# Row maxima handed over by halves of a head group, split on GpSimd, and a shorter lead of maximum units

## The reference

```
q = (x @ Wq.T).reshape(B, S, H, hd)      # B=4, S=1024, H=16, hd=8; k and v alike, q and k rotated
scores = jnp.einsum('bhqd,bhkd->bhqk', q, k) / math.sqrt(hd)
attn = jax.nn.softmax(scores, axis=-1)   # needs the maximum of each row of 1024 scores
ctx = jnp.einsum('bhqk,bhkd->bhqd', attn, v)
x = x + ga * (ctx @ Wo.T)
h = layernorm(x) * (1 + cb) + sb
_, idx = jax.lax.top_k(silu(h @ rw1 + rb1) @ rw2 + rb2, 2)     # routing to two of 8 experts
x = x + gb * (h + sum over the two experts of weight * (silu(h @ we1 + be1) @ we2 + be2))
```

## Time and profile before

| | us |
|---|---|
| median of 3 runs | 1115.19 |
| lowest and highest run | 1113.39, 1119.62 |
| span of the profiled execution | 1115.6 |
| busy: TensorE, VectorE, ScalarE, GpSimd | 905.9, 817.5, 726.9, 346.0 |
| first maximum unit on VectorE | 113.38 |
| first score matmul of the steps | 163.62 |
| first tile of the experts | 899.30 |

### The profile page before, as it was taken

How to read it: one execution, slowest core, us unless ns; L and a number is a source line. 1 busy time by engine, 2 the same in 40 slices (tenths; PEclk the granted TensorE clock), 3 DMA queues, 4 the chain that set the end, 5 groups by cost and what they waited for, 6 DMA issues and landing times. The chain is left out here.

```text
span 1115.6 us, 17986 instructions
## 1 busy us (share of the span) xinstructions
PE 905.9 (81%) x5934; PEld 362.1 (32%) x5934; DVE 817.5 (73%) x1141; ACT 726.9 (65%) x1580; POOL 346.0 (31%) x598
## 2 busy tenths in 40 slices
PE   2354459999999989898988988898898769869982
PEld 1222012222222222221212221222222168859972
DVE  3886988999999988877998798789871025613366
ACT  0043018888888878777887877788788646526651
POOL 1333000000000262043035205223323327666883
PEclk9667559999999989988998998899999779968997
DMA  4054430404402000071000000100000012112353
GB/s 123 0 196 179 162 129 1 149 16 152 158 25 105 30 2 29 23 198 49 1 30 6 25 30 25 44 1 30 1 1 13 27 44 61 54 60 68 102 146 111
DMA packets 57049, 72.69 MB, mean 65 GB/s; under 512 B 9504, under 2 KB 37664, under 8 KB 56960
## 3 DMA queue, kind: packets, MB, share of 16 engines
q1 hardware_dynamic: 52416, 62.21, 17.3%
q0 software_dynamic: 4544, 9.35, 2.4%
HBM read 30.08 MB, written 41.06 MB: 64 GB/s over the span
## 5 line engine op out<-in xcount | busy, mean ns | idle before, releaser
L860 DVE TENSOR_REDUCE half_max<-ps_max 128x2 f32<-128x1024 f32 x512 | 601.7, 1219 | 90.7 <-PE ps_max L676 71.6
L791 ACT ACTIVATE probs<-ps_scores 128x512 f32<-128x512 f32 x1024 | 540.1, 603 | 112.2 <-PE ps_scores L697 99.0
L710 PE MATMUL ps_ctx<-probs,v_grp 128*32 128x512 f32 x2048 | 286.5, 633 | 0.7 <-ACT probs L791 0.7
L697 PE MATMUL ps_scores<-q_set,k_set 51*128 51x512 bf16 x1024 | 261.2, 398 | 27.1 <-ACT probs L791 16.0
L676 PE MATMUL ps_max<-k_set,q_set 48*128 48x512 bf16 x1024 | 195.9, 409 | 70.4 <-DVE half_max L860 57.2
L697 PEld LDWEIGHTS ps_scores<-q_set,k_set 51*128 51x128 bf16 x1024 | 68.6, 94 | 347.9 <-ACT probs L791 304.1
L613 POOL TENSOR_TENSOR ctx<-turned,inv_sum 128x128 f32<-128x128 f32 x32 | 13.1, 410 | 375.7 <-DVE inv_sum L887 375.2
L1527 ACT ACTIVATE hid<-ps_up,w_tile 128x128 f32<-128x128 f32 x312 | 89.3, 370 | 58.5 <-PE ps_up L1693 53.3
L676 PEld LDWEIGHTS ps_max<-k_set,q_set 48*128 48x128 bf16 x1024 | 51.0, 96 | 177.8 <-DVE half_max L860 156.5
L1492 POOL DMA_INDIRECT y_rows<-y,y_to x78 | 91.6, 1174 | 48.9 <-DVE y L1564 32.9
L1564 DVE TENSOR_TENSOR y<-ps_down,w_tile 128x128 f32<-128x128 f32 x78 | 22.8, 292 | 104.0 <-PE ps_down L1703 58.9
(11 more groups left out here) (197 smaller groups left out, 658.0 us busy)
## 6 DMA issues: line engine op xcount, KB each, us to landing
slots<-zero_rows SPq DMA_DIRECT2D x43, 387.0 KB, 6.0
q_terms<-parts SPq DMA_DIRECT2D x24, 256.0 KB, 2.5
k_terms<-parts SPq DMA_DIRECT2D x24, 256.0 KB, 3.2
q_set<-q_terms SPq DMA_DIRECT2D x32, 192.0 KB
k_set<-k_terms SPq DMA_DIRECT2D x32, 192.0 KB
slots_in<-slots SPq DMA_DIRECT2D x78, 64.5 KB
rows<-y_rows SPq DMA_DIRECT2D x16, 256.0 KB
w_all<-in_we SPq DMA_DIRECT2D x1, 2048.0 KB
```

Source lines behind the costliest of these rows:

```text
L697: pe.matmul(bank[:], k_set[g % SETS][operand, u, tile * P:(tile + 1) * P], q_set[g % SETS][operand, u, c * BANK:(c + 1) * BANK], start=Tru ...
L710: ins = pe.matmul(ps_ctx[32 * head:32 * head + 32, :], v_grp[g % 2][:, tile, head, :], probs[:, s % RING, head, :], start=tile == 0, stop= ...
L791: act.activation(probs[:, s % RING, place, :], ps_scores[n % BANKS_S][:], ACT.Exp, scale=float(HD) ** -0.5).then_inc(slot_taken, 1)
L860: dve.reduce_max(half_max[g % 2][:, c, 2 * u:2 * u + 2, tile], ps_max[n % 2][:].rearrange("p (r n) -> p r n", r=2), axis=AX.X).then_inc(ma ...
```

## The change

Maxima are now handed over by halves of a group: half m holds the first or the last 512 queries of group m // 2 and has 16 units. VectorE only joins the two halves of the keys (128 x 16 numbers), and GpSimd splits the result in three bf16 terms. Minus ones in `k_set` take the place of the negation. TensorE transposes 48 instead of 96 rows, 32 instead of 16 times, and waits for `rows_in` every 8 steps. Before the first step stand 16 + 12 = 28 units, and the last 14 steps have none. Some of the routing's pieces move: `turn0` and `turn1` one step later, GpSimd's `modulate` and `shift` from n = 17 to n = 21, the second scatter from n = 52 to n = 54. On VectorE the wait for the tables stands behind the 28 units.

```
 def units(s):
-    first = UNITS + LEAD + 2 * s
+    first = HALF_UNITS + LEAD + 2 * s
...
+def maximum_in(s):
+    m = (s + 5) // NT
+    return m if (s + 5) % NT == 0 and 0 < m < HALVES else None
+def split_in(s):
+    m = (s + 7) // NT
+    return m if (s + 7) % NT == 0 and 0 < m < HALVES else None
...
-ROUTE_AT = dict(zip(ROUTE, (0, 2, 5, 8, 24, 26, 29, 31, 34, 36, 45)))
+ROUTE_AT = dict(zip(ROUTE, (0, 2, 5, 8, 25, 27, 29, 31, 34, 36, 45)))
...
+            def split_maximum(m):      # GpSimd, in step order, behind norm_ctx
+                out = max_parts[m % 2]
+                pool.wait_ge(row_max_ready, m + 1)
+                link(pool.tensor_copy(out[:, :, 0, :], row_max[m % 2][:]))
+                link(pool.tensor_tensor(max_rest[:], row_max[m % 2][:], out[:, :, 0, :], ALU.subtract))
+                link(pool.tensor_copy(out[:, :, 1, :], max_rest[:]))
+                pool.tensor_tensor(out[:, :, 2, :], max_rest[:], out[:, :, 1, :],
+                                   ALU.subtract).then_inc(max_parts_ready, 1)
...
-            for n in range(UNITS):
+            for n in range(HALF_UNITS + 4):      # TensorE
                 max_scores(n)
-            turn_negated(0)
-            for n in range(UNITS, UNITS + LEAD):
+            turn_maximum(0)
+            for n in range(HALF_UNITS + 4, HALF_UNITS + LEAD):
...
+            for n in range(HALF_UNITS + LEAD):   # VectorE
+                take_max(n)
+                if n == HALF_UNITS:
+                    join_halves(0)
             dve.wait_ge(r.tables_ready, r.TABLES)
```

More of the change, by code:

```diff
@@ L474, in beside @@
     found = []
-    if (g := negated_in(s)) is not None:
-        found.append(("negated", g))
+    if (m := maximum_in(s)) is not None:
+        found.append(("maximum", m))
     if (chunk := turned_in(s)) is not None:
@@ L485, in score_slots @@
 def score_slots():
-    order = [("negated", 0)] + [(0, place) for place in range(GH)] + [(1, 0)]
+    order = [("maximum", 0)] + [(0, place) for place in range(GH)] + [(1, 0)]
     for s in range(ALL_STEPS):
@@ L586, in _ @@
             store_parts(sp, k, B - 1)
-            negated_rows(0)
+            maximum_rows(0)
             sp.wait_ge(k["parts_stored"], 16 * 2 * len(TERMS))
             per_group = 9
[L590 to L595, removed]
+            for m in range(1, HALVES):
+                g = m // 2
+                if m % 2 == 0:
+                    clear_slots((g - 1) * per_group, per_group)
+                    if g == 8:
+                        load_weights()
+                maximum_rows(m)
+                if m % 2 == 0 and g + SETS - 1 < NG:
                     sp.wait_ge(set_used, g)
@@ L622, in step @@
                     norm_ctx(chunk)
+                if (m := split_in(s)) is not None:
+                    split_maximum(m)
                 b, n = route_time(s)
@@ L716, in add_ctx, with turn_maximum @@
                 ins.then_inc(ctx_added, 1)
[L718 to L722, removed]
+            def turn_maximum(m):
+                bank = bank_of(("maximum", m))
+                pe.wait_ge(max_parts_ready, m + 1)
+                pe.transpose(bank[:].bitcast(BF16)[0:GH * 3 * HALF_NT, 0:P],
+                             max_parts[m % 2][:].rearrange("p h c t -> p (h c t)"),
                              k["ident16"][:]).then_inc(slot_ready, 1)
@@ L747, in step @@
                 for what, n in beside(s):
-                    if what == "negated":
-                        turn_negated(n)
+                    if what == "maximum":
+                        turn_maximum(n)
                     elif what == "turned":
@@ L821, in step @@
                 for what, n in beside(s):
-                    if what == "negated":
-                        copy_negated(n)
+                    if what == "maximum":
+                        copy_maximum(n)
                     elif what == "turned":
@@ L861, in take_max, with join_halves @@
                                ps_max[n % 2][:].rearrange("p (r n) -> p r n", r=2), axis=AX.X).then_inc(max_taken, 1)
[L863 to L881, removed]
+            def join_halves(m):
+                g, tiles = m // 2, slice(m % 2 * HALF_NT, (m % 2 + 1) * HALF_NT)
+                dve.wait_ge(max_taken, HALF_UNITS * (m + 1))
+                if m >= 2:
+                    dve.wait_ge(max_parts_ready, m - 1)
+                dve.tensor_tensor(row_max[m % 2][:], half_max[g % 2][:, 0, :, tiles], half_max[g % 2][:, 1, :, tiles],
+                                  ALU.max).then_inc(row_max_ready, 1)
             def invert_sums(chunk):
```

68 lines of the change are left out of this document (32 added, 36 removed).

## The result

| | before | after |
|---|---|---|
| median of 4 runs each, us | 1114.29 | 1084.88 |
| lowest and highest run | 1110.68, 1119.62 | 1084.09, 1089.81 |
| span of the profiled execution | 1115.6 | 1083.2 |
| first exponential | 164.29 | 138.85 |
| last exponential ends | 888.67 | 857.67 |

The ratio is 0.974 (95% interval 0.971 to 0.978): 29 us faster, where 26 were forecast. The spans differ by 32.4 us: 0.46 stand in the preparation, 25.0 in the lead, 5.6 in the 256 steps (724.4 to 718.8 us from the first exponential to the end of the last) and 1.4 in the experts.

A forecast was written before the change was run, and what follows sets the result against it. VectorE bounds the lead, TensorE and ScalarE set the steps' pace, and handovers and experts add to it. Terms -24.8 + 0 - 4.1 + 3.0 = -25.9 us on a span of 1115.6 gave a median of 1089 us, range 1083 to 1097.

The forecast's parts named there:

- The lead: Ahead of the first exponential: no table wait, 16 units fewer and a shorter break bring first scores to 138.9; -24.8 us.
- Term (a): Start of the lead: VectorE waits only for GpSimd's tables; without that it starts at 108.62 instead of 113.38, -4.76 us.
- Free steps at no cost: Steps without maxima fall from 22 to 14; plain steps take 2.39 us with or without maxima, so 0 us.
- The handovers: Extra time where maxima are handed over: 15 costing 29.3 us become 31 costing 25.2, so -4.1 us (bounds -11 and +18).
- the choice: VectorE's choice of experts meets a handover three times, 2.2 us each on top: 6.6 us, bounds 3 and 10.
- more comes back: Rival: handovers at 0.49 us, choice of experts at 1.5, no wait at `turn0`, so 1081 us; chance 0.14.
- The 4.5-us stalls go: Three handovers beside GpSimd's row work lose their 4.5 us, since GpSimd is idle when VectorE joins there.
- GpSimd's chain: Four linked instructions between join and TensorE's transpose: cost nothing, but no slack; each 0.1 us more costs up to 3.1 us.
- the rivals' lateness: GpSimd's chain late at each of 31 handovers: by 0.9 us, 1117 us, chance 0.05; by 1.9 us, 1148 us, chance 0.05.
- The estimate from the page's figure: GpSimd's chain at twice VectorE's 0.19 us an instruction: 1.8 instead of 1.25 us, the sum some 12 us worse.
- turn0: TensorE waits about 1 us for GpSimd's `h` at `turn0`, three times: +3 us, bounds 0 and 8.
- SyncE: Issuing of weights starts about three steps later, rows behind it still in time: 0 us, up to +3 once.

The follow-up runs named there:

- experiment 1: Kernel before with only VectorE's wait for the routing tables moved behind its 44 unit maxima; first scores at 159.41 us, span 1116.7 us, run once.
- experiment 2: Kernel after with 44 maximum units ahead of the first exponentials instead of 28; ratio 0.988 to the kernel before.
- 8: Kernel after with 26 units ahead instead of 28, GpSimd's split and the transpose one step later; ratio 0.983 to the kernel before.
- experiment 3: Kernel after with the four split instructions of each half back on VectorE, halves and lead kept; ratio 1.000 to the kernel before.
- 4: Kernel after with GpSimd's modulate and shift back at slot 17 and the router's first two turns at 24 and 26; ratio 0.978 to the kernel before.
- 10: The kernel after, unchanged, measured a second time; ratio 0.975 to the kernel before, runs from 1083.6 to 1090.0 us.
- 11: Kernel after with the third batch's scatter issued behind the last step; last eight steps 19.52 us, time 1096.0 us, run once.
- experiment 5: Kernel after with one GpSimd split instruction repeated twice more, the chain 0.56 us longer; span 1081.0 us, run once.
- experiment 12: Kernel after with each batch's indirect transfers spread over steps, first eight one a step, second eight two a step; ratio 0.958 to the kernel before, 1068.5 us.
- experiment 7: Kernel after with matmuls that nobody reads added in the last 14 steps to keep TensorE busy; ratio 0.973 to the kernel before.

## Why the prediction was right, point by point

- **The lead** (-24.8). Right: -25.0 with the preparation taken off. Term (a) is shown by experiment 1, the 1.13 us a unit by experiments 2 and 8. Rows and tables were in time.
- **Free steps at no cost.** Right: plain steps kept 2.39, and experiment 2 gave almost nothing back.
- **The handovers** (29.3 to 25.2). The mechanism held and the size was off: I took a fifth of the way from 0.49 to 1.2, 0.6 each, and measured 0.49 at 22 of 31; the choice cost 1.0, 1.0 and 1.6 over a plain handover, not 2.2. So 17.6, and 11.7 us came back instead of 4.1, more even than the rival *more comes back* had (9.6). One join alone is below what the bank and the copy cost anyway.
- **The 4.5-us stalls go.** Right, and experiments 3 and 4 show both of its conditions: the split off VectorE, and off the shift's place in GpSimd's queue. The prediction gave only one of them, and the second was met by the diff's slot 21. The reason given by the Trainium skill (GPSIMD Engine Reference, "Key points"), that instructions with two SBUF inputs collide, covers the join. Experiment 3's casts have one SBUF input and were held up too, 0.65 us, so that half of the rule is not all of it; the page also names a two-port mode, and no run here shows whether the casts ran in it.
- **GpSimd's chain**, nothing, with "no slack". The cost was right, the reason wrong: the slack is 0.64 us. I compared the chain's end with TensorE's arrival and did not ask what TensorE waits for next. Of the rivals' lateness, 0.9 and 1.9 us a handover, 0.64 would have cost nothing. The estimate from the page's figure has a slip: 0.55 us more in the chain at 31 handovers is 17 us, not 12, and by the measured slack it would have cost nothing.
- **turn0** (+3). Too high: waits of 0.37 us each, 1.1 in all.
- **SyncE** (0). Right: the weights were issued from 452.58 to 469.4, the rows behind them at 474.51, in time.
- **What was not in the sum**: the last group, +6.1 us. The prediction had named the half clock only as something that shorter stalls might spare. The change moves the scatter's stall against the steps, and TensorE stays at half clock for the rest. Experiments 10 and 11 show where it sits and that the scatter makes it; why 31.05 here and 24.9 in before and in experiment 5 is open. With the handovers' -11.7 it makes the -5.6 of the steps; what other chunks lost and won by up to 1 us each cancels. It took away most of what the handovers gave over the forecast, so it is luck that the total came out nearer to the forecast than its terms.

## What to carry to other kernels

A chain on another engine has the slack of what comes last behind the engine that waits for it; lengthen it by a known amount and look, as the trace alone gave a bound that was too small twice. Small linked instructions should stand where the long elementwise work of the other engine, or of the same queue, is not running: the place in time was worth as much here as the engine. And look at the dear groups that a change leaves alone: the scatters, which this change only moved a little, cost three groups of eight steps some 10 us each, and a new place in the program gave 19 us back.

## What the runs showed of the hardware

- Linked instructions of 128x16 take 0.17 us on VectorE, one each 0.21, and 0.20 to 0.22 us on GpSimd, one each 0.28.
- Beside GpSimd's 0.70-us instructions three of VectorE's SBUF instructions took 0.65 instead of 0.17, two with one SBUF input and one with two (experiment 3).
- Beside or just behind eight indirect transfers in a row, 1.26 us apart, TensorE and ScalarE stood idle in a way that no instruction of this program explains. ScalarE's longest idle time at the six rows of after was 3.2, 1.9, 1.9, 3.2, 3.2 and 1.6 us, and up to 4.5 in experiment 12; at its rows of five and three it was 1.0 at most. What stalls them is open; the trace counts them as "issue" or "remote". The packets of the two instruction queues do not explain the longest one: none starts between 472.7 and 496.9, and the stall ends at 486.05 (experiment 12).
- After such a stall, with no maxima left, TensorE stayed at the 1.2 GHz level for the last 22 us of after's steps, and a step of 2.39 us took 3.69. In the same stretch it was back at 2.4 GHz after 3.4 us in before and 10 in experiment 2, with nothing added, and in experiment 7 within 10 us with added matmuls.
